# A 1-core adaLN block with a sparse FFN: a new opening and end of the attention part, and the first tiles' rows gathered one DMA at a time

## The reference

```python
mod = (silu(c) @ wmod)                      # six vectors of 512: sa, ca, ga, sb, cb, gb
ga, gb = sign * maximum(abs(.), 0.25)
h = layernorm(x) * (1 + ca) + sa
x = x + ga * (tanh(h @ B.T) @ C.T + D * h)
h = layernorm(x) * (1 + cb) + sb
scores = sigmoid(h @ gate_w.T); top 2 of 8 experts by scores + bias, weights normalised
out = sum over the 2 experts of weight * (silu(h @ W1) * (h @ W3)) @ W2
shared = (silu(h @ sw1.T) * (h @ sw3.T)) @ sw2.T
x = x + gb * (out + shared)
```

## Time and profile before

| what | value |
|---|---|
| median of 3 runs | 583.18 us (582.14 to 585.02) |
| the profiled execution's own time | 589.56 us |
| its span, from first to last instruction | 587.9 us |
| PE busy | 547.9 us (93%), 3176 matmuls |
| VectorE, ACT, GpSimd busy | 303.7 us (52%), 178.2 us (30%), 260.7 us (44%) |
| chain that ended last | PE 77%, GpSimd 8%, issue 5%, VectorE 4%, DMA 2% |

### The profile page before, as it was taken

One profiled execution on the slowest core, in us unless ns is written; L12 is line 12 of the kernel. 1 busy time (PEld: TensorE's weight loads), 2 busy tenths in 40 slices (PEclk: granted clock), 3 DMA queues, 4 the chain that ended last, 5 costly groups with the idle time before them and its releaser, 6 DMA issues.

```text
span 587.9 us, 11157 instructions
## 1 busy us (share of the span) xinstructions
PE 547.9 (93%) x3176; PEld 494.7 (84%) x3177; DVE 303.7 (52%) x633; ACT 178.2 (30%) x343; POOL 260.7 (44%) x219
## 2 busy tenths in 40 slices
PE   5986799999999898999999999999999999679995
PEld 2655788998899897899999999999999999579994
DVE  3589876686687567433222232222222222457886
ACT  1242345345524432123222332222322223112220
POOL 1598876667665527442053420162633002451331
PEclk9998999999999999999999999999999999798999
DMA  8988244332232578556266762548484223672644
GB/s 307 394 297 317 72 186 173 127 115 81 89 144 105 200 260 272 206 195 225 89 191 236 254 227 91 168 144 321 143 321 141 73 71 106 180 215 78 190 144 142
DMA packets 38040, 107.18 MB, mean 182 GB/s; under 512 B 4224, under 2 KB 4224, under 8 KB 36992
## 3 DMA queue, kind: packets, MB, share of 16 engines
q1 hardware_dynamic: 28288, 54.44, 26.8%
q0 software_dynamic: 9728, 52.43, 25.9%
HBM read 76.19 MB, written 30.67 MB: 182 GB/s over the span
## 4 chain that ended last, share of the span: by engine, by line
PE 77%; POOL 8%; issue 5%; DVE 4%; DMA 2%; another core or an unknown queue 1%; ACT 1%; SPq 0%; DVEq 0%; ACTq 0%; POOLq 0%
PE bank L922 14%; PE bank L923 13%; PE bank L924 13%; PE bank L938 7%; PE bank L936 7%; PE bank L937 7%; PE bank L905 5%; PE bank L943 4%; PE bank L874 2%; PE bank L876 2%; PE bank L875 2%; PE bank L883 1%; POOL xs_rows L601 1%; DMA x_all<-wmod 1%
## 5 line engine op out<-in xcount | busy, mean ns | idle before, releaser
L922 PE MATMUL bank<-whi,thi 128*128 (+1 forms) x416 | 140.9, 339 | 0.0
L923 PE MATMUL bank<-wlo,thi 128*128 (+1 forms) x416 | 136.1, 327 | 0.0
L924 PE MATMUL bank<-whi,tlo 128*128 (+1 forms) x416 | 135.6, 326 | 0.0
L531 POOL TENSOR_TENSOR wlo<-raw,whi 128x1408 f32 (+3 forms) x24 | 79.6, 3331 | 85.9 <-DMA whi<-w_all 74.4
L1596 DVE TENSOR_TENSOR gbuf<-s,bank 128x352 f32<-128x352 f32 x52 | 27.1, 521 | 112.2 <-ACT s L849 107.5
L936 PE MATMUL bank<-whi,gth 128*128 (+1 forms) x204 | 80.7, 396 | 3.3 <-DVE wlo L1320 2.0
L938 PE MATMUL bank<-whi,gtl 128*128 (+1 forms) x204 | 80.5, 395 | 0.0
L922 PEld LDWEIGHTS bank<-whi,thi 128*128 128x128 f32 x416 | 80.0, 192 | 0.0
L923 PEld LDWEIGHTS bank<-wlo,thi 128*128 128x128 f32 x416 | 79.9, 192 | 0.0
L937 PE MATMUL bank<-wlo,gth 128*128 (+1 forms) x204 | 79.8, 391 | 0.0
L924 PEld LDWEIGHTS bank<-whi,tlo 128*128 128x128 f32 x416 | 79.6, 191 | 0.0
(11 more groups left out here) (199 smaller groups left out, 982.5 us busy)
## 6 DMA issues: line engine op xcount, KB each, us to landing
raw<-w_all POOLq DMA_DIRECT2D x8, 2176.0 KB, 9.3
whi<-w_all POOLq DMA_DIRECT2D x16, 704.0 KB
h<-xs_rows SPq DMA_DIRECT2D x36, 256.0 KB
ys_rows<-tmpa SPq DMA_DIRECT2D x36, 256.0 KB, 2.0
x_all<-wmod SPq DMA_DIRECT2D x6, 1024.0 KB, 8.5
whi<-w_all POOLq DMA_DIRECT2D x8, 768.0 KB, 4.8
hs_rows<-h SPq DMA_DIRECT2D x8, 512.0 KB, 3.0
h<-hs_rows SPq DMA_DIRECT2D x16, 256.0 KB
```

Source lines behind the costliest of these rows:

```text
L531: pool.tensor_tensor(wlo[:, bass.ds(off + (SH + a), b - a)], raw[:, a:b], whi[:, bass.ds(off + (SH + a), b - a)].bitcast(F32), ALU.subtrac ...
L922: pe.matmul(dst, xh[:, j, a], wh, start=(m == 0), stop=False)
L923: pe.matmul(dst, xh[:, j, a], wl, start=False, stop=False)
L924: mm = pe.matmul(dst, xl[:, j, a], wh, start=False, stop=(m == KD - 1))
```

## The change

Four parts.

1. PE multiplies zeros ahead of the first modulation product.
2. Opening: the rows of pairs 1 and 2 are normalised by ACT (`normalise`), for which GpSimd computes the negative mean times the root as well (`first_root`); for pair 2 that comes ahead of the second layernorm's root of pair 0. C times ga is now VectorE's. VectorE takes the statistics of pair 2 ahead of the addition to x, and `first_weights(2)` comes after the first `gbuf` of pair 0.
3. End of the A pipeline: PE transposes the `h2` of pair 7 one iteration earlier; ranks and route of pairs 6 and 7 come ahead of other work; GpSimd issues the first two rounded weight loads ahead of `scatter` of pair 6 instead of after it; `table_rest` moves from step 2 of B, after `tlo`, to step 1, after `gbuf`.
4. `gather_first(t)` becomes `gather_first(t, k)`, one DMA, issued after each `gather` of c = 3 to 6.

```diff
@@ PE, opening @@
+            pe.wait_ge(pchain, 3)
+            for n in range(4):
+                pe.matmul(bank[7][:, :], zrow[:, 0:P], zrow[:, :], start=True, stop=True)
             pe.wait_ge(s_silb, KD)
             modulation(0)
@@ GpSimd, opening @@
+            def first_root(it, lo):
+                pool.wait_ge(s_st1, it * 2 + 2)
+                if lo > 0:
+                    pool.wait_ge(s_mone, 1)
+                    pool.tensor_tensor(neg1[:, :], mv1[:, :, 0], mone[:, :], ALU.mult).then_inc(s_neg1, 1)
+                pool.tensor_tensor(ve1[:, :], mv1[:, :, 1], eps_t[:, :], ALU.add).then_inc(s_ve1, 1)
+                pool.wait_ge(s_ve1, it + 1)
+                if lo > 0:
+                    pool.wait_ge(s_t, it * 2)
+                pool.tensor_tensor(rs1[:, :], ve1[:, :], mhalf[:, :], ALU.pow).then_inc(s_rs1, 1)
+                if lo > 0:
+                    pool.wait_ge(s_neg1, it)
+                    pool.wait_ge(s_rs1, it + 1)
+                    pool.tensor_tensor(nm1[:, :], neg1[:, :], rs1[:, :], ALU.mult).then_inc(s_nm1, 1)
...
             pool.wait_ge(s_ga, 1)
             pool.wait_ge(l_attn, 32)
-            for n in range(KN):
-                pool.tensor_tensor(cga[:, n, :], cga[:, n, :], mods[:, 2, :], ALU.mult).then_inc(s_cga, 1)
@@ VectorE, opening @@
-            normalise(1, 1)
+            dve.wait_ge(s_ga, 1)
+            dve.wait_ge(l_attn, 32)
+            for n in range(KN):
+                dve.tensor_tensor(cga[:, n, :], cga[:, n, :], mods[:, 2, :], ALU.mult).then_inc(s_cga, 1)
+            states_low(0)
             dve.wait_ge(s_chi, 1)
             dve.wait_ge(s_cga, KN)
             dve.tensor_tensor(clo[:, :, :], cga[:, :, :], chi[:, :, :].bitcast(F32), ALU.subtract).then_inc(s_foldc, 1)
-            states_low(0)
@@ GpSimd, end of A @@
+                if lo == NP + 2:
+                    hi_part(0, lambda: pool.wait_ge(q["A", "up"], NT))
+                    hi_part(1, lambda: None)
                 if routes(lo, hi):
                     scatter(it - 4, 0)
                 if lo == NP + 2:
-                    hi_part(0, lambda: pool.wait_ge(q["A", "up"], NT))
-                    hi_part(1, lambda: None)
                     scatter(it - 3, 1)
@@ VectorE, step() @@
-                if sec == "B" and i * 2 + j == 2:
-                    table_rest()
...
                 dve.tensor_tensor(gbuf[:, 0:F], s1[:, :], bank[3][:, 0:F], ALU.mult).then_inc(q["S", "g"], 1)
+                if sec == "B" and i * 2 + j == 1:
+                    table_rest()
@@ GpSimd, gathers of the tail @@
             for j in range(2):
                 gather(CB, j)
-            for t in range(NB):
-                gather_first(t)
-                if t % 2:
-                    for j in range(2):
-                        gather(CB + 1 + t // 2, j)
-            with pool.Fori(CB + 1 + NB // 2, NP) as c:
+            for c in range(CB + 1, NP):
                 for j in range(2):
                     gather(c, j)
+                    n = (c - CB - 1) * 2 + j
+                    if n < 2 * NB:
+                        gather_first(n // 2, n % 2)
```

More of the change, by code:

```diff
@@ L711, in high, with high_a @@
                 act.activation(xbh[:, j, :], src[:, :], ACT.Copy).then_inc(q["S", "xhi"], 1)
+            def high_a(p, lo):
+                act.wait_ge(s_h2T, p + 1)
+                if lo > 3:
+                    act.wait_ge(q["A", "up"], p * 2)
+                for j in range(2):
+                    act.activation(xah[:, j, :], h2_bank(lo, j)[:, :], ACT.Copy).then_inc(q["A", "xhi"], 1)
             def hidden(p, j, lo):
@@ L747, in turned, with normalise @@
                                    ACT.Copy).then_inc(s_thi, 1)
+            def normalise(it):
+                act.wait_ge(s_nm1, it)
+                act.wait_ge(s_tT, it)
+                act.wait_ge(s_xa, it * 2)
+                for j in range(2):
+                    xt = x_all[:, bass.ds(it * 2 + j, 1), :].rearrange("p a d -> p (a d)")
+                    act.activation(tbuf[:, j, :], xt, ACT.Identity, bias=nm1[:, j:j + 1],
+                                   scale=rs1[:, j:j + 1]).then_inc(s_t, 1)
             def states(p, lo):
@@ L767, in body @@
                     p = it - 3
-                    act.wait_ge(s_h2T, p + 1)
-                    if lo > 3:
-                        act.wait_ge(q["A", "up"], p * 2)
-                    for j in range(2):
-                        act.activation(xah[:, j, :], h2_bank(lo, j)[:, :], ACT.Copy).then_inc(q["A", "xhi"], 1)
+                    if lo < NP + 2:
+                        high_a(p, lo)
                     if lo > NP:
@@ L809, in _ @@
             turned(0, 1)
+            normalise(1)
             magnitude(2)
@@ L1041, in body @@
                     up("A", it - 3, 1, 0)
+                if lo == NP + 1:
+                    pe.wait_ge(s_h2, NT)
+                    pe.wait_ge(q["A", "xlo"], NT - 2)
+                    pe.wait_ge(q["A", "glo"], NT - 3)
+                    for j in range(2):
+                        mm = transposes(h2_bank(lo, j), h2[:, j, :])
+                    mm.then_inc(s_h2T, 1)
                 if lo == NP + 2:
+                    ranks(it - 4)
                     turn(0, 0, bank[6])
@@ L1114, in step @@
                 up("S", i, j, off, [NW + 1, NW + 2] if sec == "B" else need_up)
+                if first:
+                    ranks(NP - 1)
                 if early:
@@ L1358, in body @@
                     turned_low(it - 1, lo)
[L1359 to L1364 removed]
+                if live(3, lo, hi) and lo < NP + 2:
+                    lows_a(it - 3, lo)
+                if lo == 2:
+                    first_stats(it, lo)
+                    first_aggr(it, lo)
                 if live(2, lo, hi):
@@ L1452, in body @@
                     low_a(it - 3, 1, lo)
-                between(*range(KM + 1, KR))
+                if lo < NP + 2:
+                    between(*range(KM + 1, KR))
             body(0, 0, 0)
```

99 lines of the change are left out of this document (46 added, 53 removed).

## The result

The changed kernel takes **592.5 us** (median of 4 runs, 590.71 to 594.92) against 584.1 us for the one before (4 runs, 582.14 to 587.17): **slower by 1.4%, ratio 1.0142, 95% interval 1.0079 to 1.0205** (the interval leaves out no change, but not a loss of 2%). The forecast was 580.0, with 589.5 as the upper end. The profiled execution, one of the four, took 594.92 us, with a span of 593.3; the one before took 589.56 and is not among the four beside it.

What follows compares the result with a forecast made beforehand. PE's own work bounds the expert section; only opening, end of A and tail can move. 589.56 - 7.5 - 4.9 - 12.2 + 18.5 = 583.5 us profiled, 577.1 to 583.5 timed, middle 580.0; range 573 to 589.5.

Steps and rivals of the forecast that it cites:

- Part 1, zeros: First modulation products: zeros raise PE's clock, 0.83 to 0.43 us each; about 1.85 us gained, ends 0 and 2.7.
- Part 2, opening: Chain from ga to the first h2 shortens as work leaves GpSimd and VectorE; -7.5 us together with the zeros, ends -5 and -9.3.
- 1.85 + 3.0 + 2.9: Opening, up to the guard of gb: zeros, two multiplies off GpSimd, row operations off VectorE; 7.7 us at best, 6.2 taken.
- Part 3, end of A: End of A pipeline: PE's waits near 198 and 234 go, last scatter ends about 4 us sooner; net -4.9 us, ends -3 and -6.3.
- The 1.7 us of half clock: End of A: most of the 1.7 us that half clock costs after PE's idle before 234.61 was to go.
- Part 4, late steps: Tail: two steps that begin late, behind groups of ten and eight gathers, should go; 12.2 us gained at most.
- the 6.4 us: Profiled execution above the median of runs: outside any change (577.1) or late steps only under the profiler (583.5); middle 580.0 taken.
- Part 4, the row wait: Tail: VectorE waits four times for rows of a third DMA landing 3.6 us after issue; +18.5 us.
- The slower one: Rival for the tail: late steps are only the profiler's, so timed runs keep just the new wait; 589.3 us, chance 0.20.
- The rival of the opening: Opening: another chain, PE's products or data, comes up behind GpSimd's, only 2.7 of 7.5 us arrive; about 585, chance 0.13.
- The rival of sooner rows: Tail: third DMA lands in about 2.6 us, so the wait costs 14.5; 573 us, chance 0.15.
- that rival: Opening: the zeros don't raise PE's clock; +1.85 us, 582, chance 0.10.

Runs made afterwards that it cites:

- firsts ahead: Changed kernel with each single gather of a first tile issued ahead of the gather it stood behind; 575.30 us, ratio 0.9985 to the kernel before.
- The waiting GpSimd: firsts ahead, plus GpSimd waiting with pair 1's additions until VectorE has written pair 0's second normalised rows; 573.35 us, ratio 0.9951 to the kernel before.
- the left-out adds: firsts ahead with 510 of 512 columns of GpSimd's D*h additions for pair 1 left out; no run time given, guard of gb 4.1 us earlier.
- both edits at the end of A: firsts ahead with two weight loads behind pair 6's scatter and table_rest behind tlo; 578.03 us, or 576.29 with the GpSimd wait as well.
- raw load behind: firsts ahead with two weight loads and the 2.2 MB raw load behind pair 6's scatter; 579.48 us, and 578.58 with table_rest behind tlo too.

## Why the prediction was wrong, point by point

- **What bounds the kernel.** Right that only the opening, the end of A and the tail can move; from the mark near 249 to 497 both profiles take 247.7 us.
- **Part 1, zeros: 1.85 forecast, 0.7 measured** at the guard of ga. The pace was nearly right (0.46 for 0.43). PE's second product ended 1.5 earlier, limited by data as forecast (it waited 0.91 and 0.29 us), and of the 1.5 VectorE's L1508 ahead of the guard lost 0.9: it fell beside GpSimd's L628 and took 3.03 us for 2.14. The bound of 2.7 was too high as well: only six products were slow, 6 x 0.40 = 2.4.
- **Part 2, opening (with part 1): 7.5 forecast, 1.4 measured.** This is the step that failed first. I added up what leaves GpSimd and what leaves VectorE as if the two engines ran side by side, and put their contention at 1.2 us in a sentence beside the sum. It belonged in it, and larger: L1470 alone grew by 1.95 us on the way to the guard of gb (by 3.1 in the profile of the firsts ahead, 4.51 against 1.40). Of the terms 1.85 + 3.0 + 2.9 the profile has 0.7 + 0.1 + 0.9. The 3.0 was lost for a second reason, too: I had counted GpSimd's added operations at 0.3 each and half in a gap, but the root of pair 2, 1.8 us, stands whole ahead of pair 0's. The 12.8 us "fixed" after the guard of gb were not fixed either, but 14.2: L547 grew from 2.73 to 3.79. The waiting GpSimd and the left-out adds show the contention by experiment; the split of the rest is read from one pair of profiles.
- **Part 3, end of A: 4.9 forecast, none measured** (-0.7 in the pair compared, +0.3 in the mean of the profiles). The 1.80 at 198 went, `table_rest` gave 1.80 back at 223.91, as forecast (1.6). But the scatter didn't come earlier. I took the releaser named in the row for the one that ended the 12.03 us. The route's last index was there 2.1 us before the scatter, which should have told me to look at its other semaphore, the reload's. That was readable in the profile of before, and so was the DMA share of 0.88 and 0.91 from 203 to 213. The 1.7 us of half clock did not go either: the same wait for `xs` rows stayed (2.81 for 2.77), and with it the 0.66; whether the clock falls after it differs from profile to profile.
- **Part 4, late steps: 12.2 forecast, right where they exist.** In the profiles compared they went. In timed runs they cost about 10 us in some sets and nothing in others (585.25 against 575.65 for one kernel). My three ways of counting the 6.4 us, all or none or the middle, missed this: they differ by set, not between profile and timed run. The middle took 3.5 us off the sum; the changed kernel's profile stood only 2.4 above its median.
- **Part 4, the row wait: +18.5 forecast, 18 measured** (1.0314 x 576.63 is 18 over before, where no late step hides it). In the profile it is 18.4. That it fits so well is luck in part, for two errors cancel. From issue to use the third DMA took 4.40, 3.66, 3.67 and 4.78 us, 4.1 in the mean and not 3.6, and at 3.7 PE was 4.0 late and not 4.8, so the stretch from the rows to PE's next step was put some 0.8 too long. The slope was right: 1.1 us more of landing, 1.2 more of PE's wait.
- **The sum** missed by 583.5 against 594.9 in the profiled execution: 11.4, of which 6.1 are part 2 with part 1, and 5.6 part 3 (4.9 not won, 0.7 lost). The tail stands as forecast, 5.9 for 6.3.
- **The rivals.** The slower one had the right sign, and its place (the row wait) is what made the kernel slower; its condition, late steps only under the profiler, is not what the runs show, and its 589.3 counted the opening and the end of A as won. The rival of the opening (2.7 of 7.5 arrive) was nearest there, with a wrong mechanism. The rival of sooner rows fell: 3.7 to 4.8, not 2.6 us. (The estimate of 2.6 us from the Trainium skill's formula, DMA: Bandwidth & Descriptors, section "Anatomy of one DMA — SWDGE (gpsimd) path", is not what this kernel sees for the third of three DMAs of 256 KB; here the measurement decides.) The zeros raised PE's pace, so that rival fell too.

## What to carry to other kernels

Before removing a wait, look up when every input of the waiting instruction was there: the releaser named may not be the last one, and a load moved out of a crowded stretch crowds the next. Do not add up savings on VectorE and GpSimd that overlap in time; find the pairs of instructions that lengthen each other, and consider a wait that keeps them apart. Issue a DMA that needs nothing new ahead of those that wait for an index, and where two kernels differ by a stall that comes and goes, time them in one set of runs and compare each part by its mark, in more than one profile.

## What was unexpected

- A wait added on GpSimd (3.05 us idle) made the kernel faster: 0.9951 of before with it, 0.9985 without (another set), and within one set 576.29 against 578.03 us.
- The late steps: the same program at 575.65 and 585.25 us in two sets on one chip, within 3 us in the one and 5 in the other, and the changed kernel at 592.5 and 594.3.
- Removing a 1.8 us stall ahead of a longer one did not pay: with both edits at the end of A the idle 6.16 us in one piece were followed by five us at a granted clock of 0.50, and the pair of versions timed in one set lost 2.9 us. That the stall's removal alone did it is not shown: the same edit on top of the raw load behind gave 0.9 us.
